# A decoder layer in one kernel: self-attention's last steps moved into cross-attention, down weights loaded in one piece, scatter names prepared a slot ahead

## The chip, the cores and the metric

The kernel runs on one core of a Trainium2 chip. The time is the device's, in microseconds, the median of the runs shown. The engines are TensorE (PE, its weight loads PEld), VectorE (DVE), ScalarE (ACT), GpSimd (POOL) and SyncE (SP). SP only issues transfers; ACT and POOL issue some too.

## The reference

```python
x = x + attn(layernorm(x))            # x: (32, 64, 256); 16 heads of 16; 8-bit activations, ternary weights
x = x + xattn(layernorm(x), ctx)      # ctx: (32, 64, 128); 16 heads of 128; rmsnorm of q and k
x = x + ffn(layernorm(x))             # 8 experts, the best 2 of each token
in attn, bitlinear: x_norm = rmsnorm(x, g); scale = 127 / max|x_norm|; round, matmul, scale back
logits = xf @ router_w.T
top_v, top_i = top_k(logits, 2); probs = softmax(top_v)
g = einsum('th,efh->etf', xf, gate_w); u = einsum('th,efh->etf', xf, up_w)
y = einsum('etf,ehf->eth', silu(g) * u, down_w)
out = einsum('te,eth->th', combine, y)
```

## The kernel before, in words

The 2048 tokens lie as 16 tiles of 128 rows in x_sb. Three stages follow each other, each a block of its own with one hand-written order of work for every engine; engines meet by semaphores, and each engine works strictly in its order.

**Self-attention** is a pipeline over steps t = -4 to 22. In step t tile t+4 is quantised (front, integers on VectorE, quantise on ScalarE), tile t+3 is turned (turn), t+2 projected, the scores of t+1 are computed, and tile t gets probabilities and outputs. Pairs of tiles go on from there, named by a lag: pair(t, 2) is the pair j with 2j + 2 = t. Gained and squares have lag 2, out_scale 3, turn_out 4, project_out and residual 5, second_stats 6, h_low 7, turn_hidden 8. So steps 16 to 22 hold only what is left of pairs 4 to 7: gains and norm, quantising, output projection, residual, second layer norm, the split of h into two 16-bit halves and its turn into hT. Beside it, two jobs prepare cross-attention: ten splits of weights and context (split_high on ScalarE, split_low on GpSimd, in odd steps), and the product of Wv and Wo for two heads at a time (value_weights on TensorE into bank g1, value_high on ScalarE, value_low on VectorE, lag 2, so in even steps; outputs(t) waits for value_low because it uses the same bank).

**Cross-attention** runs over steps N = -9 to 32; m = N + 9 counts from 0. Up to m = 31 a step makes query and key of two heads for four tiles (TensorE six and three products each; ScalarE squares and copies; VectorE the low halves), from N = -1 also scores, softmax and outputs. Heads 0 to 15 use hT's first group (pairs 0 and 1); the next group is needed at m = 8. From m = 1 it also splits the expert weights into 16-bit halves, piece by piece, in DRAM w_hl.

**Experts.** Layer norm, router, top two, and a list of 39 slots of 128 (token, expert) rows each. Rows of h go to DRAM h_rows. Slot n: gather(n) on GpSimd brings the rows, turn_rows(n) on SP turns them, gate_up(n) on TensorE, silu on ScalarE, product on VectorE, hidden_high and the low half, turn_hidden(n) on SP, and three slots later down(n - 3) and result(n - 3), whose y scatter(n - 3) adds into DRAM token_out by an indirect transfer. The order on TensorE is gate_up(n), down(n - 3). GpSimd's scatters wait for each other's landing, as two slots may hold the same token. Before each scatter GpSimd copies the slot's column of names to f_to (L1398) and does a small addition (L1404) that lets the copy settle.

The loads at the start of this stage, in SP's queue: router, gate and up weights (11 MB), x_sb into token_out (L1344, x_saved), down weights of experts 0 to 2 (L1328 to L1332). Those of experts 3 to 7 can't be loaded yet: their place in arena holds hp (the rows for h_rows) and the routing's buffers (tmp, hits, names_of). ScalarE issues them after slot 1 (L1328 to L1332 again), once routing is done. SP signals experts_in after turn_hidden(2), and down(0) waits for it.

## Time and profile before

| | |
|---|---|
| median of 3 runs | 913.35 us (912.81 to 914.47) |
| profiled execution, in all | 915.99 us |
| its span | 914.2 us |
| TensorE, VectorE, ScalarE, GpSimd busy | 761.9, 609.6, 494.4, 388.5 us |
| self-attention ends, cross-attention's first instruction | 229.50, 229.79 us |
| expert stage from | 601.6 us |
| slot loop's first gate | 655.71 us |
| last scatter issued | 900.49 us |

Times inside a trace are microseconds from the span's start. A busy share is an average over stages with different limits; which engine counts has to be read stage by stage.

### The profile page before, as it was taken

The page shows a single profiled execution, that of the slowest core. Times are in us where ns is not written, and L with a number is a line of the kernel's source. Part 1 is how long each engine was busy: PE and PEld are TensorE (multiplying, and loading weights), DVE is VectorE, ACT ScalarE, POOL GpSimd, SP SyncE. Part 2 cuts the span into 40 slices and gives each one's busy share as a digit, 9 for nine tenths or more (in the row PEclk, how much of TensorE's full clock was granted, in tenths as well). Part 3 has the DMA queues.
Part 4 walks back from the last instruction along what each step waited for, and adds up shares of the span by engine and source line. Part 5 has one row for each costly group of instructions (what it writes and reads, how often), then busy time and mean ns, then how long its engine had stood idle before and what let it go on. Part 6 is the DMA issues. An engine that isn't in the chain of part 4 may idle for free. (4 is left out here: it accounts for less than half of the span.)

```text
span 914.2 us, 27602 instructions
## 1 busy us (share of the span) xinstructions
PE 761.9 (83%) x11185; PEld 542.4 (59%) x11185; DVE 609.6 (67%) x1070; ACT 494.4 (54%) x924; POOL 388.5 (42%) x446
## 2 busy tenths in 40 slices
PE   0499989883798999999999978983659999999990
PEld 0488878872344666666656556753436777776760
DVE  6788999755588989999999988877622333333320
ACT  0688877663576777677767764632123333333330
POOL 0132222213246555555555565500315666666632
PEclk9998999975899999999999998996788999999995
DMA  9111000000465433333334443069597988998974
GB/s 324 59 33 42 27 26 26 26 3 1 127 202 158 141 114 122 118 118 118 124 118 130 135 125 93 5 240 400 178 248 122 144 145 145 140 145 143 142 104 109
DMA packets 141290, 112.37 MB, mean 123 GB/s; under 512 B 88656, under 2 KB 121552, under 8 KB 140976
## 3 DMA queue, kind: packets, MB, share of 16 engines
q1 hardware_dynamic: 127952, 92.78, 37.0%
q0 software_dynamic: 7488, 10.23, 8.0%
q10 hardware_dynamic: 5728, 7.60, 2.6%
q8 instruction: 93, 1.52, 0.7%
q14 instruction: 29, 0.24, 0.1%
HBM read 63.13 MB, written 29.10 MB: 101 GB/s over the span
## 5 line engine op out<-in xcount | busy, mean ns | idle before, releaser
L1577 DVE SCALAR_TENSOR_TENSOR hid<-psu,hid 128x688 f32<-128x688 f32 x39 | 34.1, 875 | 127.6 <-PE psu L1648 121.3
L1178 PE MATMUL xbank_a<-arena,x_o 128*128 128x256 f16 x768 | 96.4, 276 | 7.0 <-DVE x_o L1003 5.3
L1178 PEld LDWEIGHTS xbank_a<-arena,x_o 128*128 128x128 f16 x768 | 71.7, 99 | 27.2 <-DVE x_o L1003 16.7
L1665 PE MATMUL fbank<-arena,hidT 128*128 (+1 forms) x663 | 84.5, 277 | 3.8 <-issue 3.4
L1083 PE MATMUL xbank_qk<-arena 128*128 128x512 f16 x336 | 83.5, 385 | 4.9 <-DVE x_gains L988 3.9
L1648 PE MATMUL psg<-wgu,f_xT 128*128 x468 | 78.6, 320 | 9.0 <-ACT hid L1434 5.8
L1665 PEld LDWEIGHTS fbank<-arena,hidT 128*128 128x128 f16 (+1 forms) x663 | 65.1, 99 | 23.3 <-issue 12.8
L849 POOL TENSOR_TENSOR x_pf<-x_sc,x_rden 128x512 f32<-128x512 f32 x32 | 33.4, 1043 | 106.2 <-DVE x_rden L1026 106.2
L1648 PE MATMUL psu<-wgu,f_xT 128*128 x468 | 76.0, 313 | 0.0
L1441 ACT CAST hid_hl<-hid 128x688 f16<-128x688 f32 x39 | 29.8, 765 | 78.9 <-DVE hid L1577 73.7
L1405 POOL DMA_INDIRECT token_out<-f_y,f_to x39 | 62.5, 1603 | 17.6 <-issue 17.3
L889 ACT ACTIVATE sqq<-xbank_qk 128x512 f32<-128x512 f32 x56 | 33.4, 597 | 63.7 <-PE xbank_qk L1083 63.7
L1648 PEld LDWEIGHTS psg<-wgu,f_xT 128*128 128x128 f16 x468 | 43.9, 100 | 34.8 <-issue 10.1
L1434 ACT ACTIVATE hid<-psg 128x688 f32<-128x688 f32 x39 | 29.0, 745 | 59.2 <-PE psg L1648 52.9
L1648 PEld LDWEIGHTS psu<-wgu,f_xT 128*128 128x128 f16 x468 | 46.4, 99 | 23.7
L1580 DVE TENSOR_TENSOR hid_hl<-hid,hid_hl 128x688 f16<-128x688 f32 x39 | 34.2, 877 | 35.0 <-ACT hid_hl L1441 35.0
L1389 POOL COPY f_at<-f_from_all 128x1 uint32<-128x1 uint32 x39 | 22.1, 567 | 75.1 <-DVE f_from_all L1556 45.9
L538 PE MATMUL bank_pt<-cst,sp 64*64 64x64 f32 x1024 | 42.6, 242 | 13.3 <-ACT pT L299 11.8
L1083 PEld LDWEIGHTS xbank_qk<-arena 128*128 128x128 f16 x336 | 28.5, 98 | 36.3 <-DVE x_gains L988 4.1
L1003 DVE SCALAR_TENSOR_TENSOR x_o<-xbank_o,x_o 128x512 f16<-128x512 f32 x55 | 37.8, 687 | 16.5 <-ACT x_o L900 16.5
L538 PEld LDWEIGHTS bank_pt<-cst,sp 64*64 64x64 f32 x1024 | 38.3, 154 | 15.9 <-issue 13.1
L218 POOL TENSOR_SCALAR kd<-cst,deq 128x128 f32<-128x128 f32 x16 | 10.4, 650 | 86.2 <-PE bank_g L584 57.6
(266 smaller groups left out, 1897.2 us busy)
## 6 DMA issues: line engine op xcount, KB each, us to landing
arena<-in_wx SPq DMA_DIRECT2D x51, 256.0 KB, 3.8
wgu<-w_hl SPq DMA_DIRECT2D x2, 5504.0 KB, 25.1
ao<-key_norms SPq DMA_DIRECT2D x64, 128.0 KB, 3.7
w_hl<-cT SPq DMA_DIRECT2D x26, 256.0 KB, 2.1
w_hl<-x_pair SPq DMA_DIRECT2D x25, 256.0 KB, 3.3
ao<-in_wx SPq DMA_DIRECT2D x10, 256.0 KB, 3.3
w_hl<-ao SPq DMA_DIRECT2D x10, 256.0 KB, 2.8
x_sb<-in_x SPq DMA_DIRECT2D x4, 512.0 KB, 9.8
```

Source lines behind the costliest of these rows:

```text
L538: last = nc.tensor.matmul(pt[rows, n * S:(n + 1) * S], sp[i % 2][rows, 8 * part + n, :], cst[rows, IDENT + S * b:IDENT + S * b + S], start ...
L849: nc.gpsimd.tensor_tensor(pf[:, :, :], sc[n % 2][:, :, :], rden[n % 2][:, :].unsqueeze(2).to_broadcast([P, 2 * GT, S]), ALU.mult).then_inc ...
L889: nc.scalar.activation(sqq[h % 2][:, :], query_bank(h), ACT.Square, scale=1.0 / (H_UP * W_UP)).then_inc(sq_done, 1)
L1003: nc.vector.scalar_tensor_tensor(out=o_hl[h % 2][:, 1, :].rearrange("p (b n) -> p b n", b=2), in0=ob_of(h)[:, :, 0:RW], scalar=1.0 / P_UP, ...
L1083: last = nc.tensor.matmul(query_bank(h), wq[:, a, k, f:f + D2], hT[:, g, b * NCH + k, :], start=(j == 0), stop=(j == len(terms) - 1))
L1178: last = nc.tensor.matmul(acc[t // 2][:, (t % 2) * C:(t % 2 + 1) * C], o_hl[h % 2][:, a, at:at + P], wvo[:, b, e, :], start=(e == 0 and j ...
L1405: nc.gpsimd.indirect_dma_start(out=dram["token_out"], out_offset=bass.IndirectOffsetOnAxis(ap=to[:, 0:1], axis=0), in_=y[n % 2][:, :], in_ ...
L1441: nc.scalar.copy(hid_hl[n % 2][:, 0, 0:FF], hid[n % 2][:, :]).then_inc(s["hh_high"], 1)
L1577: nc.vector.scalar_tensor_tensor(out=h3, in0=psu[:, :].rearrange("p (c n) -> p c n", c=2)[:, :, 0:FH], scalar=HID_UP / (H_UP * W_UP), in1= ...
L1580: nc.vector.tensor_tensor(hid_hl[n % 2][:, 1, 0:FF], hid[n % 2][:, :], hid_hl[n % 2][:, 0, 0:FF], ALU.subtract).then_inc(s["hh_low"], 1)
L1648: last = nc.tensor.matmul(bank[:, c * 512:c * 512 + FH], xT[n % 2][:, b * NCH + k, :], wgu[:, bass.ds(e, 1), at:at + FH].rearrange("p a n ...
L1665: last = nc.tensor.matmul(ps[n % 2][:, 0:C], hidT[n % 3][0:rows, a, f, :], wd[0:rows, bass.ds(e, 1), at:at + C].rearrange("p a n -> p (a n)"),
```

## The change

Three things are done, and memory is laid out anew for them.

1. The routing's buffers leave arena: masks gets memory of its own; hits and names_of lie over x_sb (VectorE therefore waits for x_saved before it writes hits); hp lies over the slot loop's work buffers (hidT, hid, xT). ScalarE saves x as its first act, and after the routing's exponential it issues all eight experts' down weights, then loads the activation table of silu. SP has neither any more; down(0) waits for down_in. TensorE does 28 idle products ahead of the slots instead of 20.
2. f_to becomes two buffers. scatter_names(n) does copy and settling one slot ahead, behind scatter(n - 1).
3. Self-attention's steps end at 15. What steps 16 to 22 did is done by functions of the same content in cross-attention: gained, squares, scale, and statistics of pair 5 before its first step, the rest at fixed places in steps m = 0 to 6. Their buffers lie over k_hl, which is allocated around both stages. TensorE no longer waits for the gains; at N = -1 it waits for all of hT. Value weights move from lag 2 to lag 1, so from even steps to odd ones, and their last pair to step 15.

```diff
-        steps = range(-4, NT + 7)
+        steps = range(-4, NT)
...
-                    if pair(t, 2) is not None:
-                        value_high(pair(t, 2))
+                    if pair(t, 1) is not None:
+                        value_high(pair(t, 1))
...
-                    if pair(t, 2) is not None:
-                        value_low(pair(t, 2))
+                    if pair(t, 1) is not None:
+                        value_low(pair(t, 1))
...
-                    need(pe, vo_low, passed(t, 2))
+                    need(pe, vo_low, passed(t, 1))
...
-                    if pair(t, 2) is not None:
-                        value_weights(t, pair(t, 2))
+                    if pair(t, 1) is not None:
+                        value_weights(t, pair(t, 1))
...
+                def gained_last():
+                    nc.gpsimd.tensor_tensor(ug[:, :, :], ao2[:, :, :], gain_o[:, :].unsqueeze(1).to_broadcast([P, 2, C]), ALU.mult).then_inc(ug_done, 1)
...
+                gained_last()
+                rest_low(5)
...
+                    if m == 3:
+                        rest_low(6)
+                    if m == 5:
+                        rest_low(7)
...
-                nc.scalar.preload_act_table_set("natural_log_exp_and_others")
-                act.wait_ge(g_ready, 4)
+                links = Chain(act, rest_act)
...
+                def squares_last():
...
+                squares_last()
+                second_norm(5)
+                turned_out(6)
+                rest_high(5)
+                quantise_last()
+                act.wait_ge(g_ready, 3)
...
+                    if m == 1:
+                        turned_out(7)
+                        second_norm(6)
+                    if m == 2:
+                        rest_high(6)
+                    if m == 3:
+                        second_norm(7)
+                    if m == 4:
+                        rest_high(7)
...
-                dve.wait_ge(g_in, 32)
...
+                def scale_last():
...
+                def residual_out(j):
...
+                second_stats(5)
...
-                dve.wait_ge(g_ready, 4)
+                turned_hidden(4)
+                hidden(5)
+                scale_last()
+                dve.wait_ge(g_in, 32)
+                nc.vector.scalar_tensor_tensor(out=gains[:, 2:3], in0=gains[:, 0:1], scalar=1.0 / CTX_UP, in1=gains[:, 1:2], op0=ALU.mult, op1=ALU.mult).then_inc(g_ready, 1)
+                dve.wait_ge(g_ready, 3)
...
+                    if m == 0:
+                        integers_last()
+                    if m == 1:
+                        second_stats(6)
+                    if m == 2:
+                        hidden(6)
+                    if m == 3:
+                        second_stats(7)
+                    if m == 4:
+                        hidden(7)
...
+                    if m == 0:
+                        residual_out(6)
+                    if m == 1:
+                        turned_hidden(5)
+                    if m == 2:
+                        residual_out(7)
+                    if m == 4:
+                        turned_hidden(6)
+                    if m == 6:
+                        turned_hidden(7)
...
+                def turn_hidden(j):
+                    if j > 4:
+                        pe.wait_ge(hl_done, j - 4)
+                        pe.wait_ge(hT_done, j - 4)
...
+                                last = nc.tensor.transpose(bank_ht[:, :].bitcast(F16)[:, n * P:(n + 1) * P], hp[:, a, l, k * P:(k + 1) * P], identh[:, :])
+                    last.then_inc(ht_done, 1)
...
+                def project_rest(j):
...
+                            last = nc.tensor.matmul(bank_wo[:, a * C:(a + 1) * C], zoT[:, a, k, :], w_int[:, NCH + k, :], start=(k == 0), stop=(k == NCH - 1))
+                    last.then_inc(wo_done, 1)
...
+                turn_hidden(4)
+                turn_out(6)
...
+                    if N == -1:
+                        pe.wait_ge(hT_done, 4)
+                        pe.wait_ge(xo_done, 4)
...
+                    if m == 0:
+                        project_rest(6)
+                    if m == 1:
+                        turn_out(7)
+                    if m == 2:
+                        project_rest(7)
+                    if m == 4:
+                        turn_hidden(6)
+                    if m == 6:
+                        turn_hidden(7)
...
+                    if m == 0:
+                        turn_hidden(5)
...
-        spare = arena[:, 3 * DC:]
-        hp = spare[:, 0:NT * C].bitcast(F16).rearrange("p (t c) -> p t c", t=NT)
-        small = spare[:, NT * C:]
...
+        behind_x = x_sb[:, :, :].rearrange("p t c -> p (t c)").bitcast(BF16)
+        hits = behind_x[:, 0:NJ * NSLOT].rearrange("p (a n) -> p a n", a=NJ)
+        names_of = behind_x[:, NJ * NSLOT:3 * NJ * NSLOT].rearrange("p (a v n) -> p a v n", a=NJ, v=2)
...
-        to = sb("f_to", [P, 1], U32)
+        to = [sb(f"f_to{i}", [P, 1], U32) for i in range(2)]
...
-        hidT = [sb(f"hidT{i}", [P, 2, FT, P], F16) for i in range(3)]
+        turned_size, hid_size, row_size = 2 * FT * P, 2 * FF, 2 * NCH * P
+        work = sb("f_slot_work", [P, 3 * turned_size + 2 * hid_size + 2 * row_size], F16)
...
+        hp = work[:, 0:NT * 2 * C].rearrange("p (t c) -> p t c", t=NT)
...
-        def down_weights(engine, first, end):
-            part, tail = slice(first, end), (FT - 1) * C
-            engine.dma_start(wd[:, part, 0:tail], weights[0, :, part, GUC:GUC + tail]).then_inc(down_in[first > 0], 16)
...
-                sp.dma_start(dram["token_out"][0:NT * P, :].rearrange("(t p) c -> p t c", p=P), x_sb[:, :, :]).then_inc(s["x_saved"], 16)
-                down_weights(sp, 0, 3)
...
-                    if n == 2:
-                        for part in down_in:
-                            sp.wait_ge(part, 64)
-                        sp.sem_inc(s["experts_in"], 1)
...
+                def scatter_names(n):
+                    nc.gpsimd.tensor_copy(to[n % 2][:, :], to_all[:, n:n + 1]).then_inc(to_ready, 1)
+                    pool.wait_ge(to_ready, n * 2 + 1)
+                    nc.gpsimd.tensor_tensor(spent[:, :], zero[:, 0:1], zero[:, 0:1], ALU.add).then_inc(to_ready, 1)
...
                 def scatter(n):
                     if n:
                         pool.wait_ge(y_saved[(n - 1) % 2], rounds(n - 1, 2))
-                    nc.gpsimd.tensor_copy(to[:, :], to_all[:, n:n + 1]).then_inc(to_ready, 1)
-                    pool.wait_ge(s["y_ready"], n + 1)
                     if n == 0:
                         pool.wait_ge(s["x_saved"], 16)
-                    pool.wait_ge(to_ready, n * 2 + 1)
-                    nc.gpsimd.tensor_tensor(spent[:, :], zero[:, 0:1], zero[:, 0:1], ALU.add).then_inc(to_ready, 1)
-                    nc.gpsimd.indirect_dma_start(out=dram["token_out"], out_offset=bass.IndirectOffsetOnAxis(ap=to[:, 0:1], axis=0),
+                    pool.wait_ge(s["y_ready"], n + 1)
+                    nc.gpsimd.indirect_dma_start(out=dram["token_out"], out_offset=bass.IndirectOffsetOnAxis(ap=to[n % 2][:, 0:1], axis=0),
                                                  in_=y[n % 2][:, :], in_offset=None, compute_op=ALU.add).then_inc(y_saved[n % 2], 16)
                 for n in range(-2, NSLOT + 4):
                     if there(n + 2):
                         gather(n + 2)
+                    if n == 3:
+                        scatter_names(0)
                     if there(n - 4):
                         scatter(n - 4)
+                    if there(n - 3) and n > 3:
+                        scatter_names(n - 3)
...
+                act.dma_start(dram["token_out"][0:NT * P, :].rearrange("(t p) c -> p t c", p=P), x_sb[:, :, :]).then_inc(s["x_saved"], 16)
...
+                tail = (FT - 1) * C
+                act.dma_start(wd[:, :, 0:tail], weights[0, :, :, GUC:GUC + tail]).then_inc(s["down_in"], 16)
+                act.dma_start(wd[:, :, DC:2 * DC], weights[1, :, :, GUC:EC]).then_inc(s["down_in"], 16)
...
+                    act.dma_start(wd[l * S:l * S + S, :, tail:DC], weights[l, 0:S, :, GUC + tail:EC]).then_inc(s["down_in"], 16)
+                nc.scalar.preload_act_table_set("silu_and_others")
...
-                    if n == 1:
-                        act.wait_ge(s["h_saved"], 32)
-                        act.wait_ge(s["routed"], 1)
-                        down_weights(act, 3, NE)
...
+                dve.wait_ge(s["x_saved"], 16)
...
-                idle_work(ps[1], 20)
+                idle_work(ps[1], 28)
...
-                        pe.wait_ge(s["experts_in"], 1)
+                        pe.wait_ge(s["down_in"], 64)
```

Lines that only move a buffer, and function bodies that repeat those of self-attention, are left out.

## Rows read from the trace of the kernel before

**Rows 1.** The page's part 4, the chain that ended last, share of the span by line.
```profile
DMA token_out<-f_y,f_to 17%; POOL f_to L1398 1%; PE psg L1648 1%; PE psu L1648 1%; POOL f_spent L1404 1%; PE fbank L1609 1%; PE fbank L1665 1%; DVE f_stats L58 1%; ACTq L1332 1%; DVE ao L1542 0%; DMA rows_in<-h_rows,f_at 0%; PE fbank L1601 0%; PE fbank L1588 0%; DMA f_xT<-rows_in 0%; POOLq L1337 0%
```

**Rows 2.** Chain of waits in the slot loop: start us, us, what.
```profile
700.99 0.66 POOL f_to L1398
...
702.45 4.19 DMA token_out<-f_y,f_to
```

**Rows 3.** Timeline of TensorE in the slot loop: start us, us, engine, line, what.
```profile
700.79 1.92 PE L1648 MATMUL psg<-wgu,f_xT 128*128 x12
...
704.30 2.12 PE L1665 MATMUL fbank<-arena,hidT 128*128 x17
706.36 1.92 PE L1648 MATMUL psg<-wgu,f_xT 128*128 x12
...
878.87 1.92 PE L1648 MATMUL psg<-wgu,f_xT 128*128 x12
```

**Rows 4.** Windows by stage: busy us of each engine, clock, DMA share, GB/s.
```profile
208.30:229.80 21.50, 6.01 (x39) 3.52 (x36) 11.06 (x32) 6.40 (x15) 4.65 (x4) 0.50 0.00 0
601.60:655.70 54.10, 30.83 (x200) 20.86 (x200) 43.69 (x135) 11.82 (x20) 6.55 (x10) 0.78 0.88 337
...
695.20:878.90 183.70, 183.70 (x1355) 129.53 (x1355) 57.80 (x67) 69.91 (x133) 115.44 (x191) 1.00 0.90 141
```

**Rows 5.** Chain of waits through the first slots.
```profile
655.71 2.94 PE psg L1648 x12
...
669.80 1.51 ACTq L1332
...
684.97 3.91 PE fbank L1665 x17
688.88 2.71 PE psg L1648 x12
```

**Rows 6.** Chain of waits in the drain.
```profile
886.07 3.91 DMA token_out<-f_y,f_to
...
891.00 3.65 DMA token_out<-f_y,f_to
```

**Rows 7.** Timeline of all engines at the seam of the two attentions.
```profile
206.05 2.22 POOL L232 TENSOR_TENSOR ck<-a_raw,ck 128x1024 f16<-128x1024 f32 x1 [4.96 <-ACT a_raw L336]
206.06 2.05 PE L632 MATMUL bank_g<-ao,wvT_raw 128*128 128x256 f32 x4 [0.31 <-issue]
...
209.69 0.69 DVE L495 SCALAR_TENSOR_TENSOR arena<-bank_g,arena 128x512 f16<-128x512 f32 x1 [2.80 <-ACT arena L340]
210.29 0.74 DVE L474 BATCH_NORM_STATS2 stats_o<-x_sb 128x6 f32<-128x256 f32 x2
...
229.79 1.28 ACT L938 ACT_TABLE_LOAD   x1 [3.34 <-PEq L194]
...
235.48 0.60 ACT L889 ACTIVATE sqq<-xbank_qk 128x512 f32<-128x512 f32 x1 [4.41 <-PE xbank_qk L1083]
```

**Rows 8.** Timeline of VectorE in cross-attention: in brackets idle before, and releaser.
```profile
254.15 0.69 DVE L993 TENSOR_TENSOR q_hl<-xbank_qk,q_hl 128x512 f16<-128x512 f32 x1 [0.88 <-ACT q_hl L890]
...
259.81 0.69 DVE L993 TENSOR_TENSOR q_hl<-xbank_qk,q_hl 128x512 f16<-128x512 f32 x1 [0.88 <-ACT q_hl L890]
```

**Rows 9.** Timeline of VectorE in two steps of self-attention.
```profile
126.49 1.71 DVE L416 TENSOR_SCALAR amax<-amax,floor 128x3 f32<-128x3 f32 x1
...
138.66 0.23 DVE L416 TENSOR_SCALAR amax<-amax,floor 128x3 f32<-128x3 f32 x1
```

**Rows 10.** A window at the end of the expert stage's loads.
```profile
648.00:650.00 2.00, 2.00 (x7) 0.76 (x6) 1.93 (x5) 0.00 (x0) 1.55 (x3) 0.60 0.15 44
```

**Rows 11.** Timeline of SP's queue in the expert stage.
```profile
663.77 1.42 SPq L1358 DMA_TRANSPOSE hidT<-hid_hl  x1
...
669.00 7.68 SPq L1358 DMA_TRANSPOSE hidT<-hid_hl  x1
```

**Rows 12.** Timeline of SP's queue at the kernel's start.
```profile
7.32 0.44 SPq L208 DMA_DIRECT2D ao<-in_wo  x1
```

More of the change, by code:

```diff
@@ L2 @@
 from concourse import mybir
+from collections import namedtuple
 from contextlib import ExitStack
@@ L83 @@
 SPLIT = H2 * D2 // 2
+Carry = namedtuple("Carry", "ao2 ug zo w_int zoT junk gain_o hp h per_pair mv_o stats_o wm ident16 identh wvT_raw")
 def need(engine, semaphore, count):
@@ L89, in need, with attention @@
         engine.wait_ge(semaphore, count)
-def attention(nc, sem, dram, x_sb, cst, ao, hT, wq, wk, wvo, cT, ck):
+def attention(nc, sem, dram, x_sb, cst, ao, hT, wq, wk, wvo, cT, ck, carry):
     ctx = ExitStack()
@@ new lines, in quantise_last, with turned_out @@
+                def quantise_last():
+                    act.wait_ge(so_done, 2)
+                    for a in range(2):
+                        nc.scalar.activation(ug[:, a, :], ug[:, a, :], ACT.Identity, scale=qsc_o[:, NPAIRS - 1, a:a + 1], bias=cst[:, CONSTS + 5:CONSTS + 6]).then_inc(yo_done, 1)
+                def turned_out(j):
+                    act.wait_ge(zt_done, j - 5)
+                    need(act, wo_done, j - 6)
+                    nc.scalar.copy(zoT[:, :, :, :].rearrange("p a k n -> p (a k n)"), bank_s[:, :].bitcast(BF16)[:, 0:2 * C]).then_inc(zoT_done, 1)
@@ new lines, in second_norm, with rest_high @@
+                def second_norm(j):
+                    act.wait_ge(st_done, 2 * (j - 4))
+                    links.link(nc.scalar.activation(ln_h[:, j, :], mv_o[:, j, :, 1], ACT.Ln, bias=cst[:, CONSTS:CONSTS + 1]))
+                    nc.scalar.activation(rstd_h[:, j, :], ln_h[:, j, :], ACT.Exp, scale=-0.5, bias=cst[:, CONSTS + 6:CONSTS + 7]).then_inc(rs_done, 1)
+                def rest_high(j):
+                    act.wait_ge(h_done, 2 * (j - 4))
+                    act.wait_ge(ht_done, j - 4)
+                    nc.scalar.copy(hp[:, :, 0, :], h_rest[:, :, :]).then_inc(hh_done, 1)
@@ new lines, in integers_last @@
+                def integers_last():
+                    dve.wait_ge(yo_done, 2)
+                    dve.wait_ge(zt_done, 1)
+                    nc.vector.tensor_scalar(zo[:, :, :], ug[:, :, :], MAGIC, None, ALU.subtract).then_inc(zo_done, 1)
+                def residual_out(j):
+                    dve.wait_ge(wo_done, j - 5)
+                    if j == NPAIRS - 1:
+                        dve.wait_ge(so_done, 2)
+                    for a in range(2):
+                        nc.vector.scalar_tensor_tensor(out=x_sb[:, 2 * j + a, :], in0=bank_wo[:, a * C:(a + 1) * C], scalar=deq_o[:, j, a:a + 1],
+                                                       in1=x_sb[:, 2 * j + a, :], op0=ALU.mult, op1=ALU.add).then_inc(xo_done, 1)
@@ new lines, in second_stats, with hidden @@
+                def second_stats(j):
+                    need(dve, xo_done, 2 * (j - 5))
+                    for a in range(2):
+                        c.step(nc.vector.bn_stats(stats_o[:, a, :], x_sb[:, 2 * j + a, :]))
+                    c.settle()
+                    for a in range(2):
+                        nc.vector.bn_aggr(mv_o[:, j, a, :], stats_o[:, a, :]).then_inc(st_done, 1)
+                def hidden(j):
+                    dve.wait_ge(rs_done, j - 4)
+                    dve.wait_ge(st_done, 2 * (j - 4))
+                    need(dve, hh_done, j - 5)
+                    need(dve, hl_done, j - 5)
+                    for a in range(2):
+                        nc.vector.tensor_scalar(h_rest[:, a, :], x_sb[:, 2 * j + a, :], mv_o[:, j, a, 0:1], rstd_h[:, j, a:a + 1], ALU.subtract, ALU.mult).then_inc(h_done, 1)
@@ L1310, in experts @@
                  "gate_done up_done silu_done hid_done hh_high hh_tail hh_low  y_done y_ready "
-                 "experts_in gate_up_in x_saved out_saved routed").split()
+                 "gate_up_in down_in x_saved out_saved routed").split()
         s = {n: sem("f_" + n) for n in names}
@@ L1315, in experts @@
         hid_turned = [sem(f"f_hid_turned{i}") for i in range(3)]
-        down_in = [sem(f"f_down_in{i}") for i in range(2)]
         to_ready = sem("f_to_ready")
@@ L1324, in rounds @@
             return 16 * (n // buffers + 1)
-        def down_weights(engine, first, end):
-            part, tail = slice(first, end), (FT - 1) * C
-            engine.dma_start(wd[:, part, 0:tail], weights[0, :, part, GUC:GUC + tail]).then_inc(down_in[first > 0], 16)
-            engine.dma_start(wd[:, part, DC:2 * DC], weights[1, :, part, GUC:EC]).then_inc(down_in[first > 0], 16)
-            for l in range(2):
-                engine.dma_start(wd[l * S:l * S + S, part, tail:DC], weights[l, 0:S, part, GUC + tail:EC]).then_inc(down_in[first > 0], 16)
         weights = dram["w_hl"].rearrange("l p (e n) -> l p e n", n=EC)
```

139 lines of the change are left out of this document (97 added, 42 removed).

## The prediction

> **What bounds the kernel now.** I read the page's chain first, then the stages one by one. The chain that ended last [rows 1] gives its largest share to the scatter of results into token_out, and its pieces in the slot loop [rows 2] look as if scatters set the pace: landing, copying a name, a settling operation, issue, next transfer. That is to be checked against TensorE. Its timeline in the same stretch [rows 3] starts gate_up's first group at 700.79 and again at 706.36, 5.57 us apart; and (878.87 - 700.79) / 32 rounds is 5.565 again, while the transfer of one scatter takes 4.19 us [rows 2] and that of another 3.65 [rows 6]. One of the two engines must give way to the other, and it is the scatter: it waits for y, and y for TensorE. The stage row [rows 4] agrees: TensorE is busy 183.70 of 183.70 us at full clock, GpSimd, the next, 115.44. So the slot loop is bound by matrix work, and the time lies elsewhere for this change: in three stretches where TensorE isn't full.
>
> First, the seam between the two attentions: from 208.3 to 229.8 TensorE does 6.01 us in 21.5, at half clock, with VectorE, the fullest engine, at 51% [rows 4]. Those are steps 16 to 22 of self-attention, a chain of small operations that hand over to each other. Second, the first four slots: the chain [rows 5] comes at 669.80 to ScalarE's queue, which issues down weights while TensorE stands still, reaches the first down product only at 684.97, and has matrix groups of 3.91 and 2.71 us where the loop's take 2.12 and 1.92 [rows 3]. Third, the drain: after the last slot the scatters do run one behind the other [rows 6].
>
> **The change, part by part.** All sums are made against the profiled execution (914.2 us span, 915.99 us in all). The median shown is 913.35, so 2.6 us less; I take the difference over to it unchanged.
>
> *Seam, what goes.* Cross-attention's block begins at 229.79 now [rows 7]. In the new kernel self-attention ends with step 15. Its last instruction is the tenth split on GpSimd, 206.05 to 208.27 [rows 7]. The value weights of pair 7 move from step 16 into step 15, and their four matrix products (2.05 us at this clock [rows 7]) now stand in front of outputs(15) on TensorE; ScalarE's split and GpSimd's follow that chain, so the end moves to about 210.4, the block's start to 210.7. Gone: 229.8 - 210.7 = 19.1 us. If the two microseconds hide, it is 21.
>
> *Seam, what is moved.* Of the 11.06 us on VectorE in [rows 4], some 0.7 us are value_low, now in step 15 [rows 7], and the second statistics, hidden(5) and scale_last, about 3.4 us, run before cross-attention's first step (statistics 0.74 [rows 7], their aggregation, and seven small operations). That prologue is a chain over four engines: squares and root on ScalarE about 2 us, norm 0.6, turned_out 0.6, hidden(5) 0.8, rest_high 0.6, scale_last 1.3, quantise_last 1.1. With overlaps I get 6.0 us until ScalarE takes query(0). Now it takes it 5.7 us after the block's start (235.48 - 229.79 [rows 7]), because of the gains' loading and a cold TensorE. Equal within 1 us.
>
> The other 7 us of VectorE and all of TensorE's 6.01, which at full clock are 3, go into the first seven steps. These steps last 5.66 us (254.15 to 259.81 [rows 8]). VectorE waits 0.88 us in each, once [rows 8], and TensorE less, so neither has room for all. TensorE's 3 us are paid in full; of VectorE's 7 us, 7 x 0.88 = 6 fit if they fall evenly. I take 4.0 us, with 3 and 8 as ends (8 if the two don't overlap and in-order waits add). Sum of the seam: -19.1 + 4.0 = -15.1, ends -18 and -10. ScalarE and GpSimd have room for theirs.
>
> *A rule against this part.* VectorE's scalar operation on a 128x3 tile took 1.71 us at 126.49 and 0.23 us at 138.66 [rows 9]; in the first case GpSimd was in the middle of a subtraction. The Trainium skill (SBUF — State Buffer, Who interferes with whom) says that VectorE in a two-port mode, or with two SBUF inputs, and GpSimd block each other for a whole instruction. By that rule, the trace agrees, the new GpSimd operations (gained_last and three rest_low) can each hold up a VectorE one; if all do for half their length the seam costs some 2.4 us more. Without it the sum stays as above, and the upper end of 8 us covers it.
>
> *Value weights one step earlier.* They move from even steps to odd ones. Same instructions, and on VectorE, the fullest engine there, +0.69 in odd and -0.69 in even steps [rows 7]. Cover: nothing is added, both kinds of step end on VectorE. Taken as 0; ends -3 and +3 us over seven pairs.
>
> *Expert stage, loads.* From 601.6 to 655.7 the transfers move 337 GB/s x 54.1 us = 18.2 MB [rows 4]: gate and up weights, x into token_out, h_rows, down weights of three experts. They end at 648, when the rate falls to 44 GB/s [rows 10]. The change puts the other five experts' 3.9 MB (five eighths of 8 x 128 x 6 KB) before that end. At 18.2 MB in 44.5 us (from 603.5, when they get going, to 648) = 0.41 MB per us that is 9.6 us: the load ends near 657.6. What is late next is the first gather (648.8) and its turn (652.9), now in quiet, then under load. A turn of hidden rows issued under the load of 667 to 684 held the queue 7.68 us where the one before it took 1.42 [rows 11]. But the load ends at 657.6, so the loss is bounded: 0 if the gather slips in, 5 us if the turn waits for the end. I take the first gate 3.5 us late.
>
> x's save as ScalarE's first issue: on an otherwise idle queue a transfer of the same shape (2 MB in rows of 1 KB, at 7.32) took 0.44 us to issue [rows 12]. ScalarE is first needed at 608.3, so it's free; so is the new wait of VectorE for x_saved at 637.9, which falls 34 us after the transfer starts (alone in its queue it needs 2.1 MB at even a sixth of 0.41 MB per us, 31 us). Masks and hits in other memory cost the same.
>
> *Expert stage, what goes.* ScalarE's issue between slots 1 and 2, the wait for experts_in, and the lower clock after them. Gate_up(0) to (2) and the shares take 14.1 us now (655.71 to 669.80 [rows 5]). Then a full gate_up (3.5) and down(0) at 673.3 instead of 684.97 [rows 5]: 11.7 us; down(0) takes 2.12 instead of 3.91, and the next group 1.92 instead of 2.71: 2.6 us more. Together 14.3, less 3.5 of the late gate: -10.8, ends -14.3 and -5 (turns under load for slot 1 too). The eight extra idle products end before the first gate; the activation table's early load takes 1.28 us out of slot 0, where TensorE does the shares anyway: 0.
>
> *Scatter names ahead.* In the loop: 0, since TensorE sets 5.57 us; cover is that wait. If it were gone, the copy (0.66 [rows 2]) and what follows it would count in every round, at the price that the drain shows. In the drain they are on the path: 889.98 landed, 891.00 issued, 1.02 us between [rows 6]. With names ready 0.2 to 0.5 should stay. Four such gaps: -2.7, ends -2 and -3.3.
>
> *A rule on the reading.* TensorE's 183.70 of 183.70 us busy stands on modelled ends; the constant spacing in [rows 3] doesn't. The Trainium skill (Perfetto Trace Analysis, Identifying the Most-Contended Engine) calls matmul busy time no good measure of closeness to the limit and points to weight loads; those are busy 129.53 of 183.70 us here, so by that rule the loop isn't shown to be TensorE's. It is the first rival below.
>
> **Sum.** -15.1 + 0 - 10.8 - 2.7 = -28.6: 887.4 us for the profiled execution, 884.8, so 885, for the median.
>
> **Rivals.**
> 1. *The scatter chain is the pace of the loop.* For it: [rows 1, 2]. Against: a spacing that stays at 5.565 us over transfers of unequal length [rows 3]. It would give 33 x 0.7 = 23 us more: 862.
> 2. *The first steps of cross-attention stretch.* Every step waits in order on carried operations, VectorE's 7 us added whole to TensorE's 3, the lock on top, some 12 us instead of 4: 893. For it: VectorE has only 0.9 us a step. Against: each result is asked for a step after it is made.
> 3. *The stall moves with the load.* The five experts' transfer holds gathers and turns of the first two slots 8 us instead of 3.5, TensorE goes cold again (2.6 us): 892. For it: 7.68 us of a held queue [rows 11]. Against: the load's end near 657.6.
> 4. *Slower than before.* Value weights in odd steps put TensorE's product, ScalarE's copy and VectorE's subtraction between probabilities and outputs of the same tile, in steps that also project out. If this lengthened each of the eight odd steps by more than 28.6 / 8 = 3.6 us the kernel loses. Against: the three operations take 2.05, 0.6 and 0.69 us at the seam's clock, and a step has room beside VectorE for the first two. At 5 us: 885 + 40 = 925.
> That the change doesn't do what it says holds of the names in the loop, and is in my forecast.
>
> **How the numbers follow.** Forecast as described 0.62, rival 1 0.04, rival 2 0.14, rival 3 0.14, rival 4 0.04, and 0.02 for no change. Ends of the likeliest case alone: -18 - 14.3 - 3.3 - 3 = 38.6 (875) and -10 - 5 - 2 + 3 = 14 (899); not all fall together, so I take 876 to 897, which holds rivals 2 and 3. About 0.2% (1.8 us) is what a measurement of this kernel can tell from no change. Faster 0.94, same 0.02, slower 0.04.
>
> **What would show it.** Seam: the window between the last split on GpSimd and the first query shrinks from 27 to some 6 us; steps in cross-attention's first seven near 6.2 us. Loads: transfers near 400 GB/s until about 657, first gate near 659, down(0) near 677 in 2.1 us, no ScalarE queue entry in the loop. Loop spacing still 5.57. Drain: landing to issue under 0.6 us. Wrong would be: turns late in the first slots, or a query in cross-attention that waits for VectorE by more than 1 us a step.

## The result, and the profile after

The changed kernel takes 899.35 us, median of 4 runs (897.4 to 901.22), where the kernel before took 913.91 beside it (4 runs, 912.81 to 916.1). The ratio is 0.9839, 95% interval 0.982 to 0.9858: faster by 1.6%. The forecast was 885 us with a range of 876 to 897, so the sign was right, the size was half, and the time fell outside the range. One execution of the kernel before (1494 us, in the first group of runs below) and one of before_names_ahead (1037 us) lie far above all others; the medians below count them, the ratios don't.

The profiled execution has a span of 899.4 us, 901.22 in all, against 914.2. The page's part 4, the chain that ended last by engine, now has TensorE first; before, transfers led it with 18%:

```profile
PE 25%; DMA 3%; DVE 3%; issue 1%; POOL 0%; POOLq 0%; ACT 0%; DVEq 0%; SPq 0%
```

The chain of [rows 1] had been the scatters'. GpSimd now waits for ScalarE's y in the loop (54.3 us of idle time ahead of the scatters, by the page), and the spacing is still 5.565 us, (867.47 - 678.26) / 34. Windows by stage, with the columns of [rows 4]:

```profile
207.00:219.80 12.80, 7.53 (x142) 6.47 (x140) 5.03 (x15) 5.27 (x8) 3.27 (x2) 0.77 0.00 1
596.70:656.90 60.20, 32.33 (x208) 21.58 (x208) 43.65 (x135) 13.10 (x21) 6.48 (x10) 0.78 1.00 369
656.90:678.30 21.40, 20.11 (x146) 13.45 (x147) 6.93 (x12) 6.46 (x12) 7.13 (x17) 0.90 0.58 114
678.30:867.50 189.20, 189.20 (x1396) 133.35 (x1396) 59.46 (x69) 71.89 (x136) 110.56 (x198) 1.00 0.87 141
```

The seam, timeline of all engines, against [rows 7]:

```profile
217.41 2.12 POOL L222 TENSOR_TENSOR ck<-a_raw,ck 128x1024 f16<-128x1024 f32 x1 [6.82 <-ACT a_raw L326]
219.86 0.42 ACT L955 ACTIVATE k_hl<-k_hl 128x256 f32<-128x256 f32 x1 [2.53 <-PEq L184]
...
223.58 1.15 POOL L866 TENSOR_TENSOR k_hl<-k_hl 128x512 f16<-128x512 f32 x1 [1.81 <-ACT k_hl L979]
...
223.95 0.81 DVE L1049 TENSOR_SCALAR per_pair<-per_pair 128x2 f32<-128x2 f32 x1
...
225.91 0.57 ACT L901 ACTIVATE sqq<-xbank_qk 128x512 f32<-128x512 f32 x1
```

The last split starts at 217.41 where it started at 206.05, so 11.4 us late: steps 16 to 22 are gone, but step 15 is later. Cross-attention starts at 219.86, not at the forecast 210.7. Its prologue takes 6.05 us to the first query, as worked out.

The expert stage, chain of waits, against [rows 5]:

```profile
643.87 6.65 DMA rows_in<-h_rows,f_at
650.54 6.20 DMA f_slot_work<-rows_in
...
656.97 3.62 PE psg L1818 x12
...
668.05 4.51 DMA f_slot_work<-rows_in
672.56 0.13 issue
672.69 1.92 PE psg L1818 x12
...
676.37 1.96 PE fbank L1835 x17
678.32 1.86 PE psg L1818 x12
```

A table of landmarks in the two profiled executions shows where 14.8 us came from. The root is ScalarE's first function of the expert stage. Head 20 is ScalarE's square for its query, where heads are counted on through the four groups of tiles, two a step, so that it opens step m = 10. A gate is the first group of matrix products of a slot. The prediction's 14.3 us for the first slots held 0.8 us of the group that starts with gate_up(4), which the table puts into the stretch behind it.

| | before | after | difference | gained in this stretch |
|---|---|---|---|---|
| cross-attention starts | 229.79 | 219.86 | -9.9 | 9.9 (forecast 19.1) |
| query of head 20 | 301.81 | 294.96 | -6.9 | -3.1 (forecast -4.0) |
| expert stage, root | 608.26 | 603.36 | -4.9 | -1.95 (forecast 0) |
| first gate | 655.71 | 656.97 | +1.3 | -6.2 (forecast -3.5) |
| gate_up(4) | 688.81 | 678.26 | -10.5 | 11.8 (forecast 13.5) |
| last gate | 878.87 | 867.47 | -11.4 | 0.85 (forecast 0.8) |
| end | 914.2 | 899.4 | -14.8 | 3.4 (forecast 2.7) |

**The self-attention row, read closely.** VectorE's first operation of each step (front) marks the steps. Before, then after, its timeline over one even and one odd step:

```profile
103.13 1.01 DVE L412 SCALAR_TENSOR_TENSOR u<-x_sb,mv,gains 128x768 f32<-128x768 f32 x1
114.94 1.01 DVE L412 SCALAR_TENSOR_TENSOR u<-x_sb,mv,gains 128x768 f32<-128x768 f32 x1
124.45 1.01 DVE L412 SCALAR_TENSOR_TENSOR u<-x_sb,mv,gains 128x768 f32<-128x768 f32 x1
```

```profile
107.63 1.01 DVE L402 SCALAR_TENSOR_TENSOR u<-x_sb,mv,gains 128x768 f32<-128x768 f32 x1
119.59 1.01 DVE L402 SCALAR_TENSOR_TENSOR u<-x_sb,mv,gains 128x768 f32<-128x768 f32 x1
129.70 1.01 DVE L402 SCALAR_TENSOR_TENSOR u<-x_sb,mv,gains 128x768 f32<-128x768 f32 x1
```

The odd step went from 9.51 to 10.11 us: value_low (0.68 us on VectorE) is now in it. The even step lost the value weights and is not shorter, 11.96 against 11.81; the two even steps after it are even longer, 12.84 and 13.43 against 12.17 and 12.28. TensorE's timeline of one even step shows why. Before, with value weights earlier in the step (at 83.77):

```profile
87.99 1.15 PE L538 MATMUL bank_pt<-cst,sp 64*64 64x64 f32 x32 [1.21 <-ACT pT L299]
89.07 0.62 PE L565 MATMUL bank_q<-zT,w_pad 128*128 128x128 bf16 x8
...
90.90 2.04 PE L594 MATMUL bank_g<-vb,pT 64*64 64x17 f32 x64
```

After:

```profile
86.23 0.40 PE L594 MATMUL bank_g<-k_hl 128*128 128x128 bf16 x4 [0.61 <-DVE k_hl L452]
...
90.30 1.20 PE L528 MATMUL bank_pt<-cst,sp 64*64 64x64 f32 x32 [2.02 <-ACT pT L289]
91.43 1.03 PE L555 MATMUL bank_q<-zT,w_pad 128*128 128x128 bf16 x8
...
94.79 2.04 PE L584 MATMUL bank_g<-vb,pT 64*64 64x17 f32 x64
```

With nothing between them, TensorE waits for zo (0.61 us) and then 2.02 us for ScalarE's turned probabilities, and the query projection that follows takes 1.03 us instead of 0.62: the granted clock went from 2.4 to 1.2 GHz (1.00 in the window from 86 to 90 us, 0.50 from 92 to 94). From the turned probabilities to the outputs it is 4.49 us instead of 2.91, on the path to the next front. That gives two causes to tell apart: the clock, and the placement, that is, the three operations (value_weights, value_high, value_low) now in the odd steps.

### The profile page after: what moved, and what is told of

Its sections match the earlier page's. It is cut to its first block and busy times, and to the rows that moved or that the text cites. A ratio compares the mean times of both kernels' runs of the same rounds, so it can differ in the third digit from the quotient of the medians.

```text
span 899.4 us, 27604 instructions
## 1 busy us (share of the span) xinstructions
PE 759.5 (84%) x11193; PEld 544.5 (61%) x11193; DVE 610.2 (68%) x1069; ACT 492.5 (55%) x923; POOL 381.7 (42%) x446
## 5 line engine op out<-in xcount | busy, mean ns | idle before, releaser
L1747 DVE SCALAR_TENSOR_TENSOR f_slot_work<-psu,f_slot_work 128x688 f32<-128x688 f32 x39 | 34.1, 874 | 124.0 <-PE psu L1818 124.0
L1566 POOL DMA_INDIRECT token_out<-f_y,f_to x39 | 62.2, 1594 | 79.9 <-ACT f_y L1622 54.3
L1818 PE MATMUL psg<-wgu,f_slot_work 128*128 x468 | 76.7, 315 | 9.2 <-DMA f_slot_work<-rows_in 9.2
L1835 PE MATMUL fbank<-arena,f_slot_work 128*128 (+1 forms) x663 | 82.7, 273 | 0.5 <-DMA f_slot_work<-hid_hl 0.5
L1835 PEld LDWEIGHTS fbank<-arena,f_slot_work 128*128 128x128 f16 (+1 forms) x663 | 64.4, 97 | 18.9 <-issue 8.9
L1818 PE MATMUL psu<-wgu,f_slot_work 128*128 x468 | 75.1, 310 | 0.0
L1614 ACT CAST hid_hl<-f_slot_work 128x688 f16<-128x688 f32 x39 | 29.8, 765 | 77.8 <-DVE f_slot_work L1747 77.8
L1818 PEld LDWEIGHTS psg<-wgu,f_slot_work 128*128 128x128 f16 x468 | 43.2, 99 | 33.9 <-issue 10.0
L1818 PEld LDWEIGHTS psu<-wgu,f_slot_work 128*128 128x128 f16 x468 | 46.0, 98 | 22.9
L1750 DVE TENSOR_TENSOR hid_hl<-f_slot_work,hid_hl 128x688 f16<-128x688 f32 x39 | 34.1, 875 | 32.4 <-ACT hid_hl L1614 32.4
L528 PE MATMUL bank_pt<-cst,sp 64*64 64x64 f32 x1024 | 43.1, 244 | 14.3 <-ACT pT L289 13.7
L1209 PEld LDWEIGHTS xbank_qk<-arena 128*128 128x128 f16 x336 | 28.6, 98 | 32.7 <-DVE q_hl L1099 2.5
L1217 PE MATMUL xbank_qk<-cT,wk 128*128 128x512 f16 x168 | 46.0, 383 | 0.0
```

What stands on the lines that cost most here:

```text
L528: last = nc.tensor.matmul(pt[rows, n * S:(n + 1) * S], sp[i % 2][rows, 8 * part + n, :], cst[rows, IDENT + S * b:IDENT + S * b + S], start ...
L1209: last = nc.tensor.matmul(query_bank(h), wq[:, a, k, f:f + D2], hT[:, g, b * NCH + k, :], start=(j == 0), stop=(j == len(terms) - 1))
L1217: last = nc.tensor.matmul(key_bank(h), wk[:, a, f:f + D2], cT[:, g, b, :], start=(j == 0), stop=(j == 2))
L1566: nc.gpsimd.indirect_dma_start(out=dram["token_out"], out_offset=bass.IndirectOffsetOnAxis(ap=to[n % 2][:, 0:1], axis=0), in_=y[n % 2][:, ...
L1747: nc.vector.scalar_tensor_tensor(out=h3, in0=psu[:, :].rearrange("p (c n) -> p c n", c=2)[:, :, 0:FH], scalar=HID_UP / (H_UP * W_UP), in1= ...
L1750: nc.vector.tensor_tensor(hid_hl[n % 2][:, 1, 0:FF], hid[n % 2][:, :], hid_hl[n % 2][:, 0, 0:FF], ALU.subtract).then_inc(s["hh_low"], 1)
```

## The experiments

All against the kernel before, which took 913.99 us beside the first four, 914.14 beside the second and 913.83 beside the last (medians of 11 to 17 runs):

| run | median us (range) | ratio, 95% interval |
|---|---|---|
| warm_even_steps | 891.55 (888.0 to 893.11) | 0.9751, 0.9716 to 0.9786 |
| lag_two | 890.94 (890.48 to 894.5) | 0.9765, 0.973 to 0.98 |
| before_lag_one | 923.14 (919.84 to 927.21) | 1.0111, 1.0075 to 1.0148 |
| before_new_experts | 906.95 (905.76 to 907.99) | 0.9929, 0.9903 to 0.9955 |
| before_names_ahead | 912.42 (908.16 to 914.16, and one of 1037.35) | 0.9974, 0.9955 to 0.9993 |
| late_down_half | 898.81 (898.43 to 900.19) | 0.9835, 0.9813 to 0.9858 |
| late_down_all | 904.94 (903.48 to 907.85) | 0.9906, 0.9881 to 0.993 |
| lag_two_idle | 885.92 (884.37 to 886.03) | 0.9688, 0.9666 to 0.971 |
| attentions_alone | 905.85 (903.78 to 908.62) | 0.9916, 0.9892 to 0.994 |
| lag_one_idle | 889.03 (888.4 to 891.01) | 0.9731, 0.9708 to 0.9754 |
| down_in_pieces | 898.7 (898.44 to 900.22) | 0.9839, 0.9816 to 0.9862 |
| combined | 886.23 (884.41 to 892.53) | 0.9713, 0.9681 to 0.9744 |

**Is it the lag?** Two runs: the lag taken back out of the changed kernel, and put alone into the kernel before.

```diff
+        def weights_pair(t):
+            return NPAIRS - 1 if t == NT - 1 else pair(t, 2) if t < NT - 1 else None
-                    if pair(t, 1) is not None:
-                        value_weights(t, pair(t, 1))
+                    if weights_pair(t) is not None:
+                        value_weights(t, weights_pair(t))
```

(value_high and value_low likewise; outputs waits for passed(t, 2), and for all in step 15.)

> The changed kernel, with the value weights of pairs 0 to 6 back in the even steps (lag 2), and only pair 7's in step 15. Both theories (clock, placement) want less time. Clock alone: about 6 us less in self-attention, 893 us. Placement alone: 7 x 0.6 = 4 us less, 895 us. Both: cross-attention begins near 210.5 as predicted, 9 us less, 890 us. If neither holds and the 11 us come from the carried buffers (addresses in k_hl, other waits), the time stays at 899 us.

> The kernel before, with only the value weights moved from lag 2 to lag 1; steps 16 to 22 stay. Clock and placement together: self-attention's step 15 ends 9 to 11 us later, of which step 16 gives back about 1 us, as value_weights no longer stands in it: 913.9 + 9 = 922 to 924 us. Placement alone: 918 us. If the lag isn't the cause: 913 to 914 us.

lag_two takes 890.94, 8.4 us less than the changed kernel, and before_lag_one 923.14, 9.2 us more than the kernel before. The steps of lag_two are those of before again (from 103.58: 11.94, then 9.51), and its block starts where the prediction had put it, at 211.5; its first query, in ScalarE's timeline:

```profile
217.55 0.57 ACT L904 ACTIVATE sqq<-xbank_qk 128x512 f32<-128x512 f32 x1
```

That is 8.36 us ahead of 225.91. By the medians the lag costs 8.4 to 9.2 us, and the carried buffers nothing that can be seen. By the traces, counted from the first front to the block's start, lag_two takes 187.7 us, and the attentions of the changed kernel 194.2 to 194.5 in three profiles (late_down_half, late_down_all, down_in_pieces) and 196.6 and 196.7 in two (the changed kernel and attentions_alone). Those two have a step 0 of 11.6 us, where the others have 9.3 to 9.5; no value weights stand in that step. So 6.5 to 6.8 us of the lag's cost are seen there.

**How does it cost them?** First, idle products in the emptied even steps.

```diff
+                def idle_products(t, count):
+                    need(pe, ao_done, tiles(t))
+                    for i in range(count):
+                        nc.tensor.matmul(g1[:, i % 2 * C:(i % 2 + 1) * C], wvT_raw[:, i % 2, :], wo2_raw[:, i % 2, :], start=True, stop=True)
...
                         value_weights(t, pair(t, 1))
+                    if t % 2 == 0 and 2 <= t < NT:
+                        idle_products(t, 2)
```

> The changed kernel, with two idle products of value_weights' shape in every even step from 2 to 14, at the place on TensorE where the kernel before has value_weights; nobody reads them. Clock theory: the even steps, emptied of value_weights, leave TensorE idle 0.96 + 2.02 us each and the granted clock falls, so that the rest of the step (turned probabilities, projections, turn, outputs) runs at 1.2 GHz and the step is 1.0 to 1.7 us longer. The idle products keep it up: about 5 us less in self-attention, 894 to 895 us in all, TensorE idle 2.02 us but at full clock in most even steps. Placement theory: the odd steps are VectorE's and pay 0.6 us each for value_low, the even steps gave nothing back, the clock costs nothing: 899 to 900 us.

Adding work made it 7.8 us faster than the changed kernel, more than the 5 expected; in its trace 4.45 us of that lie ahead of the first query (221.46). The same even step, TensorE's timeline:

```profile
90.36 1.15 PE L528 MATMUL bank_pt<-cst,sp 64*64 64x64 f32 x32 [0.70 <-ACT pT L289]
91.44 0.62 PE L555 MATMUL bank_q<-zT,w_pad 128*128 128x128 bf16 x8
...
93.27 2.04 PE L584 MATMUL bank_g<-vb,pT 64*64 64x17 f32 x64
```

The query projection is back at 0.62 us and the outputs start 2.91 us behind the probabilities, as before the change. The two even steps from 128.27 and 149.95 take 11.57 us each, where the changed kernel's took 12.84 and 13.43. It isn't so everywhere: the step ahead of the one shown took 13.41 us in this trace, at a granted clock of 0.62, and 9.33 in the changed kernel. The odd steps from 106 us on stay at 10.11 us.

Then idle products in the other gap of the even steps, between the scores and turn_probs(t, 1), on either lag. They write to qb behind the wait that project has anyway. lag_one_idle has both kinds.

```diff
                         scores(t + 1)
+                    if t % 2 == 0 and 2 <= t < NT - 2:
+                        idle_products(t, 3)
                     if tile(t):
                         turn_probs(t, 1)
```

> The changed kernel with lag 2 as in lag_two, and three idle products in each even step from 2 to 12 behind the scores, where TensorE waits 1.8 us for ScalarE's turned probabilities and the clock then falls in about half of the steps. Clock theory: those steps lose 1.5 us each, so 4 to 6 us less than lag_two, 885 to 887 us. If ScalarE and VectorE alone set these steps: 890.9 us as before; if the idle products stand in the way by 0.3 us a step, 893.

> The changed kernel (lag 1), with idle products at both places in the even steps: two ahead of turn_out, as in warm_even_steps, and three behind the scores, as in lag_two_idle. TensorE is then kept up in the even steps for both lags, and what is left between this kernel and lag_two_idle (885.9 us) is the placement alone: 0.6 us in each of eight odd steps by the placement theory, 890 to 891 us. If the clock was all: 886 us.

885.92 and 889.03 us. Windows of the changed kernel, then of lag_one_idle (columns as in [rows 4], the clock third from the end):

```profile
100.00:120.00 20.00, 17.02 (x420) 15.99 (x417) 17.95 (x34) 16.09 (x34) 4.55 (x4) 0.91 0.10 29
120.00:140.00 20.00, 17.02 (x386) 15.54 (x386) 18.95 (x34) 16.40 (x34) 5.74 (x5) 0.83 0.09 29
140.00:160.00 20.00, 17.02 (x420) 15.66 (x419) 17.87 (x32) 14.78 (x34) 5.54 (x5) 0.90 0.09 29
```

```profile
100.00:120.00 20.00, 19.47 (x468) 17.50 (x464) 18.70 (x36) 16.36 (x36) 5.78 (x5) 1.00 0.10 30
120.00:140.00 20.00, 18.68 (x434) 16.50 (x431) 18.79 (x38) 16.42 (x35) 5.17 (x4) 1.00 0.09 29
140.00:160.00 20.00, 18.69 (x433) 16.46 (x432) 18.76 (x36) 15.54 (x34) 5.78 (x5) 1.00 0.09 29
```

lag_two_idle is at 1.00 in most such windows too, with one at 0.83, so the placement is what is left, perhaps a little more than the difference: 889.03 - 885.92 = 3.1 us. The clock costs the changed kernel 899.35 - 889.03 = 10.3 us, and a kernel with lag 2 also 890.94 - 885.92 = 5.0; the change's own part is the difference, 5.3. 5.3 + 3.1 = 8.4, what lag_two gained.

This split is less sure than its sum. The intervals of the four ratios reach 1.7 to 3.2 us to either side. Worked out from the ratios in place of the medians, the clock's own part is 2.9 us and the placement 3.9. The traces say nearly the same: from the first front to the block's start it is 194.5 us (late_down_half and late_down_all, which have the changed attentions), 187.4 for lag_one_idle, 187.7 for lag_two and 183.4 for lag_two_idle, which makes 7.1 - 4.3 = 2.8 us for the clock and 4.0 for the placement. So both theories hold, and which part is the larger isn't settled.

Where the placement costs is seen in the fronts. VectorE's timeline over one odd and one even step of lag_one_idle, then of lag_two_idle:

```profile
113.98 1.01 DVE L402 SCALAR_TENSOR_TENSOR u<-x_sb,mv,gains 128x768 f32<-128x768 f32 x1
124.09 1.01 DVE L402 SCALAR_TENSOR_TENSOR u<-x_sb,mv,gains 128x768 f32<-128x768 f32 x1
135.65 1.01 DVE L402 SCALAR_TENSOR_TENSOR u<-x_sb,mv,gains 128x768 f32<-128x768 f32 x1
```

```profile
112.16 1.01 DVE L405 SCALAR_TENSOR_TENSOR u<-x_sb,mv,gains 128x768 f32<-128x768 f32 x1
121.68 1.01 DVE L405 SCALAR_TENSOR_TENSOR u<-x_sb,mv,gains 128x768 f32<-128x768 f32 x1
133.85 1.01 DVE L405 SCALAR_TENSOR_TENSOR u<-x_sb,mv,gains 128x768 f32<-128x768 f32 x1
```

The odd step takes 10.11 us against 9.52, and the even one 11.56 against 12.17. So where the clock stays up (1.00 and 0.94 in these two even steps), the even step does give back the 0.6 us that the odd one pays. The even step of lag 2 takes the same 12.17 us at 0.90 (kernel before, from 124.45) as at 0.97 (combined). The changed kernel's even step from 129.70 ran at 0.73 and took 12.84. Over steps 5 to 10 the two runs with idle products come out equal, 64.48 and 64.52 us. The placement's 4.0 us come from steps 1 to 4 (1.5 us, where only the odd steps differ) and from what follows the last front (2.3 us); why nothing is given back there is not shown.

**The rest, split by stage.** The two halves of the change, each with the other half as before:

> The kernel before up to cross-attention's end, with the changed kernel's expert stage (buffers, down weights, order of loads, scatter names ahead). By the prediction's terms 10.8 + 2.7 = 13.5 us less, 900.4 us. By the two traces (expert stage 6.4 us shorter up to gate_up(4), 3.4 us from there to the end) 9.8 us less, 904.1 us; then the rest of the gain, 4.9 us, is the attentions'.

> The changed kernel's two attentions with the expert stage of the kernel before. The prediction's seam term: 15.1 us less, 899 us. By the two traces cross-attention ends 4.9 us earlier, and the new expert stage alone gave 7 us: this should give 5 to 8 us less, 906 to 909 us. If it gives 15, the loss of 11 us in self-attention was an interplay with the new expert stage, which no row supports.

7.0 and 8.0 us less than before, 15.0 together, and the whole change 14.6: they add up. The half with the expert stage gave half of the prediction's 13.5 us, and less than the 9.8 read from the two traces. Within it, the names alone:

```diff
+                def scatter_names(n):
...
+                    if there(n - 3) and n > 3:
+                        scatter_names(n - 3)
```

> The kernel before, with only the scatter names prepared one slot ahead (two f_to buffers). Prediction's term: 2.7 us less, all in the drain, loop spacing 5.565 us as before: 911.2 us. The two traces put 3.4 to 4 us between gate_up(4) and the end: 910 us. If the scatter chain had been the loop's pace: 33 x 0.7 = 23 us less, 891 us.

912.42 against 914.14 us; by the ratio it is 2.4 us less, with an interval of 0.6 to 4.1, which holds the 2.7 but does not measure it. The trace shows the term itself, landing to issue on the chain in the drain:

```profile
889.74 0.27 issue
890.01 3.88 DMA token_out<-f_y,f_to
893.90 0.27 issue
```

1.02 us became 0.27, and the last six scatters are issued over 24.0 us instead of 25.2. The loop spacing is unchanged. The scatter chain as the loop's pace (23 us) is out.

**Does the load set the first gate?** The changed kernel, with the second half of the down weights, then with all of them, held back:

```diff
+                act.wait_ge(rows_turned[0], 16)
                 act.dma_start(wd[:, :, DC:2 * DC], weights[1, :, :, GUC:EC]).then_inc(s["down_in"], 16)
```

> The changed kernel, with the second half of the down weights (3 MB and the two tails) issued by ScalarE only once slot 0's rows are turned. If the load's end sets the first gate (gather 6.65 and turn 6.20 us under load against 4.09 and 2.56 before), the load pauses near 645, the first gate comes 5 to 6 us earlier, near 651, and the time falls by 3 to 6 us, as far as the turns of slots 1 to 3 don't wait under the second half in their turn. If the stall only moves: gate_up(1) or (3) waits for its turn by as much, 899 us. If the gather is slow for another reason (its first issue takes 2.28 us): no change at the first gate.

> The changed kernel, with all down weights (6 MB) issued by ScalarE only once slot 0's rows are turned. The load before it ends near 638, so gather and turn run in quiet: first gate near 650.5. The 6 MB then take 15 us at 0.41 MB per us, till near 665, and the turns of slots 1 and 2 and the gathers of 2 and 3 fall under them: 6 to 8 us of stall, 899 to 903 us. If turns aren't slowed by load: 893 us.

The first gate comes 47.5 and 47.6 us behind the root (647.69 and 647.51), as before the change (47.45) and not 53.6 as after it. So the load does set it. But the kernels take 898.81 and 904.94 us. Chain of waits of late_down_half:

```profile
645.65 2.78 DMA rows_in<-h_rows,f_at
648.43 0.02 issue
648.45 10.89 DMA f_slot_work<-rows_in
659.34 0.13 issue
659.47 3.62 PE psg L1819 x12
...
665.07 4.38 DMA f_slot_work<-rows_in
```

The turn for slot 1 takes 10.89 us under the second half of the load, and gate_up(4) stands 75.0 us behind the root; in the changed kernel it is 74.9. The gain moved whole into the next wait. In late_down_all the first turn takes 2.55 us, ScalarE's queue then holds up silu(0), and gate_up(4) comes at 82.8. The Trainium skill (DMA: Bandwidth & Descriptors, Issuing engines are not separate DMA queues) says that transfers issued by ScalarE, SyncE or GpSimd run on the same 16 DMA engines and interleave. The runs agree: the load is in ScalarE's queue, the turns are in SyncE's, and a turn takes 10.89 us under the load and 2.55 without.

**Smaller pieces, and the sum.**

```diff
+                down_weights(act, 0, 3)
...
+                act.wait_ge(rows_turned[0], 16)
+                down_weights(act, 3, 5)
                 for n in range(NSLOT + 3):
...
+                    if n < 3:
+                        down_weights(act, 5 + n, 6 + n)
```

> The changed kernel, with the down weights in five pieces: experts 0 to 2 where ScalarE has all eight now, 3 and 4 once slot 0's rows are turned, 5, 6 and 7 behind the work of slots 0, 1 and 2; down(0) waits for all. If turns wait for as long as a load lasts that is issued ahead of them: first gate 6 us earlier (47.5 us behind the stage's root activation, as in late_down_half), then waits of at most 4 and 2 us instead of one of 11, gate_up(4) some 4 us earlier, 895 us. If ScalarE's issues hold up silu, or the pieces come too late for down(0): 899 to 903 us.

> lag_two_idle with the down weights in pieces: the two act in different stages, so the sum of both: 885.9 less what down_in_pieces gains, about 882 us; 886 if the pieces gain nothing.

898.7 and 886.23 us: nothing gained on 899.35 and 885.92. Gate_up(4) comes 73.9 us behind the root, 1.0 us earlier than in the changed kernel; TensorE now waits 2.14 us ahead of gate_up(1) and 3.39 ahead of gate_up(3) in place of one long wait, and the sum is nearly the same. The best version is lag_two_idle, 885.92 us, 3.1% under the kernel before.

## Why the prediction was half right, step by step

- **Seam, what goes.** The new end of self-attention was put at 210.4 us, the block's start at 210.7. With lag 2 it starts at 211.5: the arithmetic on the steps that leave was right. The changed kernel starts at 219.86 because of the next point.
- **Value weights one step earlier: the step that failed.** "Taken as 0; ends -3 and +3 us over seven pairs" measured 8.4 to 9.2 us by the medians. The argument was that the same instructions stand in another step, that both kinds of step end on VectorE, and that one gives back what the other pays. Where TensorE's clock stays up this is what the runs show (10.11 for 9.52 us, 11.56 for 12.17). What it left out is the clock: the products that left had helped to keep it up, and in the changed kernel's even steps it fell (0.73 and 0.75 in the two from 129.70 and 152.66), so that they took 12.84 and 13.43 us and gave nothing back. That is 2.8 to 5.3 us. The prediction had this price for the seam and the first slots, but not here. The other 3.1 to 4.0 us are lost in steps 1 to 4, where the odd steps grew and the even ones stayed, and behind the last front. This was rival 4's place, at 1.1 us for each of eight odd steps and not beyond the 3.6 from which it decides.
- **Carried work** was taken as 4.0 us and measured 3.1 between the block's start and head 20. The first seven steps take 6.15 us each on average (5.59 to 7.11), where the prediction said near 6.2. Rival 2 (12 us) did not come. VectorE's 0.81 us on a 128x2 tile beside GpSimd's L866 is the kind of hold-up of [rows 9]; the allowance for it was not needed.
- **A further 1.95 us** in the rest of cross-attention is that one execution's: the same code took 305.97 to 306.84 us from head 20 to the root in four other profiles (attentions_alone, the two late_down runs, down_in_pieces), the changed kernel 308.40 and the kernel before 306.45.
- **Expert stage.** Forecast 10.8, read 6.5. The first gate was mis-sized: 6.2 us late instead of 3.5, and beyond the 5 us that were put as its bound. The load's end was put at 657.6, and that was nearly right: the rate falls at 651 already, but ScalarE's queue moves small packets until 655.8, and the DMA share stays at 1.19 to 1.47 from 651 to 655. The gather took 6.65 us, and the turn, issued at 650.54, took 6.20, with its own packets seen only from 653.0 on. So the turn too ran under the load. And rival 3 came in part: the turn for slot 3 took 4.51 us, of which TensorE waited 1.22 ahead of gate_up(3). The held-back loads show that this is one sum, the time until the load and the first turns are both through. One misreading had no effect: the queue of [rows 12] wasn't otherwise idle, as transfers went to it at 6.04 and 6.64 us too; x's save took 0.43 us to issue.
- **Drain and loop**: 3.4 us forecast as 2.7; spacing 5.565 as forecast.

On the profiled spans the forecast missed by 28.6 - 14.8 = 13.8 us: 9.2 in self-attention's end (219.86 - 210.7), 4.3 in the expert stage, 1.95 in the rest of cross-attention, less 0.9 for the carried work and 0.7 for the drain. Of the 9.2 some 2 are the long step 0 of this profile. The prediction's own worst case of the likeliest course came to 899; it was narrowed to 897 because not all ends fall together. That the measured 899.35 is nearly this worst case is luck: the value weights' term alone went far beyond its own end of 3 us.

Not settled: how the lag's cost divides between clock and placement, and over the steps, since the clock falls in other steps from one profile to the next; why step 0 took 11.6 us instead of 9.3 to 9.5 in two of five profiles of the new attentions, before any value weights.

## What to carry to other kernels

Work moved between two kinds of step is not free because its engine is the fullest on average: ask of each kind what ends it, and at which clock of TensorE, since one pays and the other may not give back. Before taking matrix products out of a step in which TensorE waits, look at the durations behind that wait; they may be what keeps the clock. A load that several queues share is one sum: holding back a part of it moved the wait here and didn't shorten it, in three runs. Whether a part would gain in a stretch in which nothing small waits for transfers was not run.

## What was unexpected of the hardware

- Idle products that nobody reads, two in each of seven even steps, took 7.8 us off the time, and three more at the next gap brought the lag-one kernel to 10.3 us less. The granted clock in 100 to 160 us rose from between 0.83 and 0.91 to 1.00. The longest single idle time of TensorE between 85 us and the end of self-attention's steps was 2.03 us in the changed kernel.
- A transfer that turns a slot's rows took 2.55 us in quiet, 6.20 under the small packets at the load's end and 10.89 under 3 MB from another engine's queue.
